# The widths of a mixture-of-experts layer's first product in steps of 16 slots instead of 32

## The chip, the cores and the metric

The kernel runs on 1 core of one Trainium2 chip. The metric is the device time of one execution in microseconds (us). Before the change three runs gave 1121.9, 1123.8 and 1128.33 us, with a median of 1123.8 us.

## The reference

The reference has two layers on x of 4 x 512 tokens with 512 channels. The first is a bidirectional recurrence with a time-dependent decay, a gated linear recurrence on its result, and a projection. The second is the same kind of conditioning followed by a mixture of 8 experts. Cut to what matters here:

```python
C = ceil(1.25 * S * K / E)            # 640 slots for each expert
probs = softmax(xr @ Wg)
gate_vals, expert_idx = top_k(probs, 2)
pos = running number of the token within its expert
kept = pos < C
dispatched = xr[dispatch_mask]        # 8 x 640 x 512
h = relu(einsum('ecd,edf->ecf', dispatched, w1))   # to 2048 hidden
expert_out = einsum('ecf,efd->ecd', h, w2)
x = x + the tokens' expert rows, weighted by their gates
```

An expert's slots beyond its number of tokens are empty. That number is known only when the kernel runs.

## The kernel before, in words

The first part of the program (`conditioning_and_routing`) computes the first layer, the conditioning and the routing for the four sequences, writes the tokens' rows into a DRAM tensor `slots` of 640 rows for each expert, and leaves each expert's number of tokens, limited to 1 to 640, in `counts`. It ends at about 370 us.

The second part (`experts`) is a loop over the 8 experts that every engine runs for itself, with semaphores between them. The hidden dimension of 2048 is cut into 16 blocks of 128. Matrices of fp32 are split into a high and a low part of type fp32r, and each product is made of three: high by high, low by high, high by low.

PE's program (`tensor_program`) is what the change touches. Within the loop over experts (L1624) it loads the expert's count into a register (L1625), and then runs a loop of 8 passes (L1630), each for two hidden blocks:

- `up` (first product, L1575 to L1577): 4 slices of the channels by 3 products into the PSUM tensor `ps_h`, for as many slots as the chosen width has. With up to 512 slots it is one body of 12 products; above, the slots are done in two parts of which the first has 320 columns, 24 products in all.
- `down` (second product, L1595 to L1597) of the hidden block before, for each tile of 128 slots that has tokens: 3 products of 512 columns into `ps_y`. It waits for the relu and the split of the hidden block, which ACT (L1702) and DVE (L1774) make. Tiles 0 and 1 are always done, tiles 2 to 4 behind a branch each (L1602).
- from the third pass on, four transposes of a tile of the next expert's rows (L1545).

The width is not a register operand of the product. PE chooses one of the bodies that the program holds, one for each width in `WIDTHS`, by nested branches on the count (`choose`, L1580 to L1587): the lower half stands behind the branch and is reached by falling through, the upper half by a jump. All bodies stand in the program one after the other, twice, since `up` is called twice in a pass. The chosen width is the smallest one that holds the count.

ACT and DVE read `ps_h` over fixed widths: 512 columns for up to 512 tokens, twice 320 for more. They also split the weights (L1676, L1679, L1734, L1737), that SP loads in pieces of 1 MB. POOL adds the finished rows into the output (L1524).

The lines that decide the bodies are:

```python
WIDTHS = range(2 * P, CAP + 1, P // 4)      # P = 128, CAP = 640
middle = (len(widths) - 1) // 2
with pe.If(count < widths[middle] + 1):
    choose(widths[:middle + 1])
with pe.Else():
    choose(widths[middle + 1:])
```

Of the kernel before, what the change touches and what calls it, by code (L numbers as in the profile page):

```python
# [24 lines left out]
P = 128  # L25
# [4 lines left out]
CAP = math.ceil(1.25 * B * T * TOPK / NE)  # L30
# [46 lines left out]
def build_program(nc, x, fside, cond, w1c, u1c, W_in, b_in, W_decay, b_decay, W_gate, b_gate,  # L77
# [3 lines left out]
    with ExitStack() as ctx:  # L81
# [18 lines left out]
        with ExitStack() as phase:  # L100
            first = conditioning_and_routing(nc, ctx, phase, ident, counts, count_sem, rows, cond_buffers, place0, load_sems,
                                     slots, out_rows, x, fside, cond, w1c, u1c,
                                     W_in, b_in, W_decay, b_decay, W_gate, b_gate, W_out, b_out,
                                     decay_bias, w2c, u2c, Wg, w1, w2)
        second = experts(nc, ctx, ident, counts, rows, count_sem, place0, load_sems, slots, out_rows, w1, w2)
        block = ctx.enter_context(nc.Block())

# [1298 lines left out]
def experts(nc, ctx, ident, counts, rows, s_count, place0, load_sems, slots, out_rows, w1, w2):  # L1406
# [32 lines left out]

    WIDE = 512  # L1440
    HALF = CAP // 2
    WIDTHS = range(2 * P, CAP + 1, P // 4)
    TURN_FROM = 2

    EVEN_ORDER, ODD_ORDER = (2, 4, 0), (3, 1)
# [88 lines left out]
    def tensor_program(pe):  # L1534
# [27 lines left out]
        def up(hidden, j, count):  # L1562
# [17 lines left out]
            def choose(widths):  # L1580
                if len(widths) == 1:
                    products(widths[0])
                    return
# [5 lines that stand above are left out]
            pe.wait_ge(s_wl1, hidden + 1)  # L1589
            choose(WIDTHS)  # L1590

# [235 lines left out]
```

How the kernel before makes its waits and increments, by code:

```python
    def wait(self):  # L69
        self.eng.wait_ge(self.sem, self.base + self.n)
# [207 lines left out]
    def sync_program(sp):  # L278
# [6 lines left out]
        def store(b):  # L285
            sp.wait_ge(s_ev_x2, TT * (b + 1))
            sp.dma_start(out_rows[b * T:(b + 1) * T].rearrange("(i p) c -> p i c", p=P), x_rows).then_inc(s_x2_out, 16)
# [4 lines left out]
        def clear_slots(first, last):  # L292
            for e in range(first, last):
                sp.dma_start(slots[e * CAP:(e + 1) * CAP, :].rearrange("(p i) c -> p i c", i=ST),
                             r2_rows[:, 0:1, :].to_broadcast([P, ST, ROW])).then_inc(s_init, 16)
        for h in range(2):
            half = slice(h * C // 2, (h + 1) * C // 2)
            sp.dma_start(f_rows[:, :, half], fside[0].rearrange("(i p) c -> p i c", p=P)[:, :, half]).then_inc(s_f_in if h else s_f_half, 16)
        sp.wait_ge(s_vec, 16 * N_VEC)
        load_x(0)
        sp.wait_ge(s_f_tp, CT)
        load_f(1)
        for n in range(4):
            load_w(n)
        sp.dma_start(wg[:], Wg.rearrange("(t p) e -> p t e", p=P)).then_inc(s_w, 16)
        sp.wait_ge(s_x_tp, CT)
        load_x(1)
        sp.wait_ge(s_f_tp, 2 * CT)
        load_f(2)
        sp.wait_ge(s_template, 2)
        clear_slots(1, NE + 1)
        sp.wait_ge(s_f_tp, 3 * CT)
        load_f(3)
        store(0)
        sp.wait_ge(s_x2_out, 16)
        load_x(2)
        store(1)
        sp.wait_ge(s_x2_out, 32)
        load_x(3)
        sp.wait_ge(s_bwd, 2 * (unit_no(1, B - 2, 1) + 1))
        sp.wait_ge(s_eukv, unit_no(1, B - 2, 1) + 1)
```

## Time and profile before

| | |
|---|---|
| runs | 1121.9, 1123.8, 1128.33 us; median 1123.8 |
| the profiled execution | 1130.62 us, span 1128.8 us |
| granted TensorE clock, mean over the span | 0.969 |
| PE busy | 1040.3 us (92%), 5034 products |
| PE weight loads busy (beside PE) | 816.5 us |
| DVE, ACT, POOL busy | 644.6, 519.7, 279.3 us |
| loop over experts | from 373.9 us to about 1109 us |

The span runs from the first to the last instruction of the profiled execution. A product's duration includes the time in which it overlaps the next one, so the rate of products is read from the distance between their starts. PEld is the loading of weights into the array, which overlaps the products. PEldq and PEq are the queue of PE: branches and register operations are shown there with their durations, and are not counted as busy time. "issue" is time in which an engine waited for nothing that the profile shows. The instruction queues (q8, q14) carry the program itself to the engines.

### The profile page before, as it was taken

What the parts mean: (1) busy time and instruction counts of PE and PEld (TensorE: products, weight loads), DVE (VectorE), ACT (ScalarE), POOL (GpSimd) and SP (SyncE); (2) the same over time, 40 slices, a digit from 0 to 9 for tenths busy, and PEclk for the clock granted to TensorE, in tenths of its full rate; (3) what the DMA queues carried; (4) which work ended last, traced back from release to release, by engine and by line L of the source; (5) the groups of instructions that cost most, each with busy time, mean ns of one, the idle gap of its engine ahead of it and who ended that gap; (6) DMA issues with size and microseconds to landing.
All of it is one profiled execution on the core that took longest, in us unless ns stands there. A gap on an engine that the chain in (4) does not pass through costs nothing.

```text
span 1128.8 us, 17219 instructions
## 1 busy us (share of the span) xinstructions
PE 1040.3 (92%) x5034; PEld 816.5 (72%) x5035; DVE 644.6 (57%) x939; ACT 519.7 (46%) x836; POOL 279.3 (25%) x232
## 2 busy tenths in 40 slices
PE   3599997999996899999999999999999999999993
PEld 2334543454455799989998999898887888899892
DVE  5899999999982333343334333555564344334551
ACT  6776774677632233343334333445553334334441
POOL 4665748634654000030002000300203002000202
PEclk9999898999988899999999999999999999999997
DMA  6991432224414422262226222634536225222521
GB/s 212 315 308 30 112 72 89 53 69 113 136 39 169 146 74 74 74 167 75 74 74 168 74 74 74 172 144 166 165 114 213 74 74 158 89 92 90 137 74 22
DMA packets 67104, 131.34 MB, mean 116 GB/s; under 512 B 4966, under 2 KB 6026, under 8 KB 67080
## 3 DMA queue, kind: packets, MB, share of 16 engines
q1 hardware_dynamic: 53856, 105.25, 26.8%
q0 software_dynamic: 13008, 25.52, 11.5%
q10 hardware_dynamic: 216, 0.28, 0.1%
q8 instruction: 12, 0.20, 0.1%
q14 instruction: 12, 0.10, 0.0%
HBM read 90.66 MB, written 35.22 MB: 112 GB/s over the span
## 4 chain that ended last, share of the span: by engine, by line
PE 64%; issue 1%; POOL 1%; DVEq 0%; DVE 0%; ACT 0%; POOLq 0%
PE ps_y L1595 11%; PE ps_y L1596 11%; PE ps_y L1597 11%; PE ps_h L1575 10%; PE ps_h L1576 10%; PE ps_h L1577 10%; PE ps_t L1545 1%; POOL out_dram L1524 1%; DVEq L1650 0%; DVE y L1797 0%; DVE hl L1774 0%; ACT y L1719 0%; DVE gate L1759 0%; DVEq L1773 0%; DVEq L1763 0%
## 5 line engine op out<-in xcount | busy, mean ns | idle before, releaser
L1575 PE MATMUL ps_h<-xh,w1h 128*128 128x320 f32 (+4 forms) x768 | 245.0, 319 | 7.7 <-issue 7.1
L1576 PE MATMUL ps_h<-xl,w1h 128*128 128x320 f32 (+4 forms) x768 | 241.3, 314 | 0.0
L1577 PE MATMUL ps_h<-xh,w1l 128*128 128x320 f32 (+4 forms) x768 | 241.2, 314 | 0.0
L1524 POOL DMA_INDIRECT out_dram<-y,token x40 | 63.8, 1594 | 642.4 <-DVE y L1797 402.2
L1774 DVE SCALAR_TENSOR_TENSOR hl<-ps_h,hh 128x320 fp32r<-128x320 f32 (+1 forms) x192 | 107.2, 558 | 191.9 <-ACT hh L1702 187.1
L1595 PE MATMUL ps_y<-w2h,hh 128*128 128x512 f32 x528 | 207.1, 392 | 0.8 <-issue 0.5
L1596 PE MATMUL ps_y<-w2h,hl 128*128 128x512 f32 x528 | 206.3, 391 | 0.0
L1597 PE MATMUL ps_y<-w2l,hh 128*128 128x512 f32 x528 | 206.1, 390 | 0.0
L1702 ACT ACTIVATE hh<-ps_h 128x320 fp32r<-128x320 f32 (+1 forms) x192 | 94.2, 491 | 234.6 <-PE ps_h L1577 231.2
L1737 DVE TENSOR_TENSOR w2l<-raw,w2h 128x512 fp32r<-128x512 f32 x127 | 87.8, 692 | 196.6 <-ACT w2h L1679 195.6
L1679 ACT ACTIVATE w2h<-raw 128x512 fp32r x127 | 80.1, 631 | 210.2 <-PE ps_y L1597 210.2
L515 PE MATMUL ps_mm<-ratios,wm 128*128 128x512 f32 x372 | 168.5, 607 | 7.2 <-DVE xT L1218 4.0
L1575 PEld LDWEIGHTS ps_h<-xh,w1h 128*128 128x128 f32 x768 | 145.5, 190 | 16.2 <-issue 10.5
L1576 PEld LDWEIGHTS ps_h<-xl,w1h 128*128 128x128 f32 x768 | 145.6, 190 | 5.0
L1577 PEld LDWEIGHTS ps_h<-xh,w1l 128*128 128x128 f32 x768 | 145.4, 189 | 2.6
L515 PEld LDWEIGHTS ps_mm<-ratios,wm 128*128 128x128 f32 x372 | 70.6, 195 | 91.5 <-issue 84.8
L1597 PEld LDWEIGHTS ps_y<-w2l,hh 128*128 128x128 f32 x528 | 99.1, 188 | 21.6
L1595 PEld LDWEIGHTS ps_y<-w2h,hh 128*128 128x128 f32 x528 | 99.2, 188 | 20.0 <-issue 2.7
L1596 PEld LDWEIGHTS ps_y<-w2h,hl 128*128 128x128 f32 x528 | 99.2, 188 | 17.0
L1734 DVE TENSOR_TENSOR w1l<-raw,w1h 128x512 fp32r<-128x512 f32 x127 | 87.6, 690 | 16.0 <-ACT w1h L1676 12.2
L1676 ACT ACTIVATE w1h<-raw 128x512 fp32r x127 | 79.2, 623 | 0.0
L1161 DVE TENSOR_TENSOR_SCAN sums_odd<-ps_decay,sums_odd 128x511 f32<-128x511 f32 x32 | 38.3, 1257 | 4.5 <-ACT sums_odd L791 4.5
(206 smaller groups left out, 1163.8 us busy)
## 6 DMA issues: line engine op xcount, KB each, us to landing
raw<-in_L_ffn_w_dram SPq DMA_DIRECT2D x64, 1024.0 KB
slots<-r_rows SPq DMA_DIRECT2D x8, 1302.5 KB, 22.6
rows<-slots SPq DMA_DIRECT2D x7, 1302.5 KB
rows<-in_x_dram SPq DMA_DIRECT2D x4, 1024.0 KB, 5.2
sums_even<-eukv POOLq DMA_DIRECT2D x8, 512.0 KB, 5.1
sums_odd<-eukv POOLq DMA_DIRECT2D x8, 512.0 KB, 5.3
out_dram<-rows SPq DMA_DIRECT2D x4, 1024.0 KB
f_rows<-in_fside_BxSxS_dram SPq DMA_DIRECT2D x3, 1024.0 KB, 6.6
```

The lines of the kernel that those rows point to most:

```text
L515: last = nc.tensor.matmul(ps_mm[:, k % 3, :], wm[:, m, dt, e * P:(e + 1) * P], ratio_of(0, b)[:, dt], start=(dt == 0), stop=(dt == CT - 1))
L1575: nc.tensor.matmul(o, w1h[:, j, dt, :], xh[:, dt, lo:hi], start=(dt == 0), stop=False)
L1576: nc.tensor.matmul(o, w1h[:, j, dt, :], xl[:, dt, lo:hi], start=False, stop=False)
L1577: last = nc.tensor.matmul(o, w1l[:, j, dt, :], xh[:, dt, lo:hi], start=False, stop=(dt == CT - 1))
L1595: nc.tensor.matmul(ps_y[:, i, :], hh[:, j, tok], w2h[:, j], start=first, stop=False)
L1596: nc.tensor.matmul(ps_y[:, i, :], hl[:, j, tok], w2h[:, j], start=False, stop=False)
L1597: return nc.tensor.matmul(ps_y[:, i, :], hh[:, j, tok], w2l[:, j], start=False, stop=last)
L1679: a.activation(w2h[:, (j + 1) % 2], raw2[:, bass.ds((c + (j + 1) // FC) % 2, 1), (j + 1) % FC] .rearrange("p o n -> p (o n)"), ACT.Copy).t ...
L1702: a.activation(hh[:, j % 2, lo:hi], ps_h[:, bank, 0:hi - lo], ACT.Relu).then_inc(s_hh, 1 if wide else 2)
L1734: v.tensor_tensor(w1l[:, j % 2], raw1[:, bass.ds((c + j // 2) % 2, 1), :, (j + 2) % FC * P:((j + 2) % FC + 1) * P] .rearrange("p o t q -> ...
L1737: v.tensor_tensor(w2l[:, (j + 1) % 2], raw2[:, bass.ds((c + (j + 1) // FC) % 2, 1), (j + 1) % FC] .rearrange("p o n -> p (o n)"), w2h[:, ( ...
L1774: v.scalar_tensor_tensor(out=hl[:, j % 2, lo:hi], in0=ps_h[:, bank, 0:hi - lo], scalar=0.0, in1=hh[:, j % 2, lo:hi].bitcast(F32), op0=ALU.max,
```

## The change

```diff
     WIDE = 512
     HALF = CAP // 2
-    WIDTHS = range(2 * P, CAP + 1, P // 4)
+    WIDTHS = range(2 * P, CAP + 1, P // 8)
     TURN_FROM = 2
```

The widths were 256, 288, ..., 640 (13) and are now 256, 272, ..., 640 (25). Only PE's program changes; those of DVE, ACT, POOL and SP are the same instruction by instruction.

PE's program at the head of the loop of 8 passes, where the search through the widths begins (L1585) and the first bodies stand. Before:

```order
L1630 UNCONDITIONAL_BRANCH
L1630 ISA
L1585 COMPARE_AND_BRANCH x4
L1570 REGISTER_ALU
L1575 MATMUL ps_h<-xh,w1h 128x256
...
L1585 UNCONDITIONAL_BRANCH
L1570 REGISTER_ALU
L1575 MATMUL ps_h<-xh,w1h 128x288
```

With the change:

```order
L1630 UNCONDITIONAL_BRANCH
L1630 ISA
L1585 COMPARE_AND_BRANCH x5
L1570 REGISTER_ALU
L1575 MATMUL ps_h<-xh,w1h 128x256
...
L1585 UNCONDITIONAL_BRANCH
L1570 REGISTER_ALU
L1575 MATMUL ps_h<-xh,w1h 128x272
```

One more branch stands ahead of the narrowest body, and the second body has 272 columns where it had 288.

The wide bodies, where 544 is the narrowest of them before and 528 after: the second part of the body (its first part has 320 columns). Before:

```order
L1577 MATMUL ps_h<-xh,w1l 128x320
L1568 REGISTER_ALU
L1575 MATMUL ps_h<-xh,w1h 128x224
L1576 MATMUL ps_h<-xl,w1h 128x224
L1577 MATMUL ps_h<-xh,w1l 128x224
```

With the change:

```order
L1577 MATMUL ps_h<-xh,w1l 128x320
L1568 REGISTER_ALU
L1575 MATMUL ps_h<-xh,w1h 128x208
L1576 MATMUL ps_h<-xl,w1h 128x208
L1577 MATMUL ps_h<-xh,w1l 128x208
```

The second part has 208 columns where it had 224, and a body with 224 stands behind it as one of its own. The whole of PE's program has 792 rows of different neighbours before and 1240 after.

## Rows read from the trace of the kernel before

**Rows 1.** The page: busy time by engine, and one line of the DMA queues.

```profile
PE 1040.3 (92%) x5034; PEld 816.5 (72%) x5035; DVE 644.6 (57%) x939; ACT 519.7 (46%) x836; POOL 279.3 (25%) x232
q8 instruction: 12, 0.20, 0.1%
```

**Rows 2.** The table by stretches: us, busy us (count) by engine, granted clock, DMA share, GB/s.

```profile
0.00:373.90 373.90, 310.04 (x1006) 164.92 (x1007) 322.28 (x421) 233.12 (x328) 211.60 (x178) 0.93 0.46 136
787.10:850.20 63.10, 61.64 (x356) 54.04 (x357) 38.15 (x60) 33.73 (x56) 8.67 (x8) 1.00 0.51 163
850.20:939.80 89.60, 89.59 (x404) 73.96 (x404) 37.88 (x59) 33.80 (x56) 8.59 (x7) 1.00 0.37 119
939.80:1046.70 106.90, 106.90 (x646) 96.75 (x646) 44.16 (x75) 39.20 (x74) 9.23 (x8) 1.00 0.33 105
```

**Rows 3.** Waits of PE, 370 to 1105 us: total us, times, longest.

```profile
PE ps_h L1575 <- issue: 7.1, 7, 3.3
```

**Rows 4.** Groups of L1575 by shape, 373.9 to 1109 us: busy us, mean ns, idle before.

```profile
L1575 PE MATMUL ps_h<-xh,w1h 128*128 128x512 f32 x64 | 25.5, 398 | 1.2 <-issue 1.2
L1575 PE MATMUL ps_h<-xh,w1h 128*128 128x352 f32 x64 | 21.2, 331 | 0.3 <-issue 0.3
L1575 PE MATMUL ps_h<-xh,w1h 128*128 128x288 f32 x64 | 19.4, 303 | 1.2 <-issue 1.2
L1575 PE MATMUL ps_h<-xh,w1h 128*128 128x224 f32 x64 | 17.4, 272 | 0.0
```

**Rows 5.** The timeline of PE: start us, us; bodies of 12 products by their ends.

```profile
796.87 0.29 PE L1575 MATMUL ps_h<-xh,w1h 128*128 128x288 f32 x1
798.45 0.39 PE L1595 MATMUL ps_y<-w2h,hh 128*128 128x512 f32 x1
...
866.65 0.39 PE L1595 MATMUL ps_y<-w2h,hh 128*128 128x512 f32 x1
869.37 0.39 PE L1575 MATMUL ps_h<-xh,w1h 128*128 128x512 f32 x1
...
962.78 0.30 PE L1575 MATMUL ps_h<-xh,w1h 128*128 128x320 f32 x1
964.53 0.27 PE L1575 MATMUL ps_h<-xh,w1h 128*128 128x224 f32 x1
965.86 0.40 PE L1595 MATMUL ps_y<-w2h,hh 128*128 128x512 f32 x1
```

**Rows 6.** Branches of the search, L1585: 377.9 to 380.9, then 385.5 to 1105 us.

```profile
L1585 PEldq COMPARE_BRANCH  x3: 215/217/2618, 377.9 to 380.8; - x3
L1585 PEldq COMPARE_BRANCH  x458: 65/202/215, 385.7 to 1101.7; - x153
```

**Rows 7.** Three searches (L1585) and the weight loads they lead to (L1575).

```profile
L1585 PEldq COMPARE_BRANCH  x3: 202/202/215, 488.9 to 489.4; - x3
L1575 PEld LDWEIGHTS ps_h<-xh,w1h x3: 188/188/188, 490.8 to 491.8; 128*128 128x128 f32 x3
...
L1585 PEldq COMPARE_BRANCH  x3: 202/202/208, 656.1 to 656.6; - x3
L1575 PEld LDWEIGHTS ps_h<-xh,w1h x1: 190/190/190, 658.3 to 658.3; 128*128 128x128 f32 x1
...
L1585 PEldq COMPARE_BRANCH  x4: 65/71/208, 798.2 to 798.6; - x4
L1575 PEld LDWEIGHTS ps_h<-xh,w1h x2: 188/188/188, 800.3 to 800.8; 128*128 128x128 f32 x2
```

**Rows 8.** The timeline of PE: the fifth expert's first product.

```profile
787.13 0.39 PE L1575 MATMUL ps_h<-xh,w1h 128*128 128x288 f32 x1 [1.06 <-issue]
```

**Rows 9.** Instruction queues in 360 to 470 us, then in 470 to the end.

```profile
q8 instruction: 4, 0.07, 0.2%
...
q14 instruction: 1, 0.01, 0.0%
```

**Rows 10.** The timeline of PE behind the long branch.

```profile
381.17 0.42 PE L1575 MATMUL ps_h<-xh,w1h 128*128 128x320 f32 x1 [0.86 <-issue]
```

## The prediction

> **What bounds the kernel now.** I read the page first: PE is busy 92% of the span, DVE 57%, ACT 46% [rows 1]. The table by stretches shows where: from 373.9 us on, where the experts run, PE is busy in practically every microsecond (89.59 of 89.6 in the stretch of the sixth expert) at a granted clock of 1.00, and DVE and ACT have half their time left [rows 2]. So a product that becomes shorter there shortens the kernel, and an instruction of PE's queue costs something only where the queue runs late. The waits of PE show that this is rare now: 7.1 us ahead of L1575, all of it "issue", in 7 places [rows 3].
>
> **Which products change.** Routing the reference's own inputs gives the eight experts 626, 770, 788, 326, 267, 495, 518 and 306 tokens, and 640 is the cap. The trace agrees: beside the 320 columns of most experts it has 64 products of each kind at 352, 288, 512 and 224 columns, 224 being the second part of 544 [rows 4]. In steps of 16 the widths become 336 for 326, 272 for 267, 496 for 495 and 528 for 518 (second part 208). 626, 770 and 788 stay at 640 and 306 at 320. Each of the four has 16 hidden blocks of 12 products that become 16 columns narrower, 192 products.
>
> What a column is worth I take from starts, since durations are pipelined. Twelve products of 512 columns go from 866.65 to 869.37, 226.7 ns each; twelve of 320 from 962.78 to 964.53, 145.8 ns; twelve of 288 from 796.87 to 798.45, 131.7 ns [rows 5]. From 288 to 512 that is 0.42 ns a column, so 6.7 ns for 16. Twelve of 224 take 964.53 to 965.86, 110.8 ns, where the line would give 105: a floor begins to show. For 208 columns I bound the saving by nothing and by 6.7 ns and take 2 ns. Sum: 3 x 192 x 6.7 ns + 192 x 2 ns = 4.3 us saved (3.9 to 5.2).
>
> **What is added on PE's queue.** The search through the widths is nested branches. By the code 640 takes three jumps now and four after; 352 and 288 have four steps and 336 and 272 five; 320 has one step more, 544 three and 528 five, 512 and 496 four both. A step that falls through takes 65 to 71 ns, one that jumps 202 to 217 ns [rows 6, 7], with some 60 ns between them. The Trainium skill (Advanced Engine Details and Errata, Control Flow Timing) gives about 108 ns for a compare-and-branch; the rows show two prices around it, and the sum by 108 ns would be lower by under 1 us. Mostly this lies beside PE's work: in the fifth expert the last branch of a search ends at 798.8 and the LDWEIGHTS that it leads to starts at 800.3; in the third expert these are 656.8 and 658.3 [rows 7]. That is 1.5 us of lead in both, so a longer search costs nothing in the steady loop. It costs where PE already waits for "issue", as the 1.06 us ahead of 787.13 [rows 8]: about seven such places by 0.13 to 0.4 us, +2 us (1 to 3).
>
> **The size of the loop.** Here the change is largest. A narrow body is 26 instructions (a register operation, twelve LDWEIGHTS and MATMUL pairs, a branch), a wide one 51. Before, a search has nine narrow and four wide bodies and 12 compares, 450 instructions; after, seventeen, eight and 24, 874. The loop over pairs of hidden blocks has two searches and 188 other instructions: 1088 before, 1936 after, and the loop over experts around it 1144 and 1992.
>
> The trace shows how PE's instructions come. Queue 8 moves 12 packets in 0.20 MB, 16.4 KB each [rows 1]; 4 of them lie between 360 and 470 us, where the loop over experts is first run, and none between 470 and the end, where only queue 14 has one [rows 9]; so 8 came before 360. Ahead of 373.9 us PE has some 1006 products [rows 2], so about 2,060 instructions with waits: about 257 to a packet. That makes the loop over experts 4.5 packets before and 7.8 after. Before, what was fetched once stayed: no packet comes on queue 8 in the last 650 us. And the fetch runs one ahead: packets come in the first pass at blocks that are entered without a stall, except where a jump overtakes them. That is the one branch of 2618 ns, between 377.9 and 380.9 [rows 6]; at ordinary 213 ns this is a stall of 2.4 us, of which PE lost 0.86 us idle plus a slow start, 1.0 us [rows 10]. All 458 later branches of a search stay at 215 ns or below [rows 6].
>
> After the change the inner loop begins in the ninth packet of PE's program and ends in the sixteenth, eight packets, and on entering its last one the fetch ahead asks for the seventeenth, a ninth. How many are kept no row says; the rows show six (five of the loop and one ahead). Nine at once is half as much again as anything the trace shows to be kept, and nothing suggests a loss or a gain below that. The price of a loss is the branch of 2618 ns. I take that nine aren't kept and that the ninth takes the place of the first, which the jump back needs in every pass.
>
> The Trainium skill (Runtime: NRT & Kernel Launch, Instruction fetch mechanics) gives PE 128 KiB, 2048 instructions, refilled in blocks of 16 KiB, and says a taken branch outside what is held stalls for a fetch. By it nine blocks don't fit. The trace agrees with the block (16.4 KB) and with the stall (2618 ns), and not with the page's sentence that only two blocks are held: five are jumped among without a fetch.
>
> **The sum for that case.**
> - Each of 56 jumps back within an expert: 2.4 us less the lead of 1.5 us [rows 7] = 0.9 us, 50 us.
> - The lead itself is eaten by the longer searches: 3 experts x 7 x 0.27 us, 3 x 7 x 0.13 and 7 x 0.4, 11 us.
> - Seven changes of expert: at the five after wide or 512-column experts and the like the lead is 489.6 to 490.8, 1.2 us [rows 7], so 1.2 us each; the two after narrow ones have none [rows 8], 2.4 us each: 11 us.
> - The first pass: both searches of the first expert now hop over several packets within 0.3 us of each other. Two stalls of 2.4 us before the very first product stand free (4.8); two more in the second search less the 1.4 us that PE's queue covered before, 3.4 instead of 1.0: +7 us.
> - Products -4.3 us, starts of experts +2 us.
>
> Together 77 us: 1130.6 of the profiled execution becomes 1208. The shown median is 1123.8, 6.8 below that execution; from it I forecast **1201 us**. Bounds of this case: if only the wide experts lose their first block, the jumps give half, +40, 1164; if a miss takes 3.4 us because the packet has not been asked for ahead, +1 us in 63 places, 1264.
>
> DVE, ACT, POOL and SP keep their instructions, and read ps_h over the same columns as before. The weights' transfers lie beside PE's work with 33 to 51% of the DMA engines busy [rows 2]; a slower PE only gives them more room. I cost these at nothing.
>
> **Rivals.**
> 1. *All blocks stay.* Then only the saving, the starts and the first pass count: -4.3 + 2 + 0 to 7, 1121.5 to 1128.5, likeliest 1127. For it: before, not one packet was fetched twice. It decides the sign: it holds if nine packets of 16.4 KB are kept, or if a packet asked for ahead never displaces one in use. Chance 0.35.
> 2. *Every block is lost in turn*, because the oldest goes first: each of the 32 passes of the wide experts pays about what the first does (7 us) and the narrow ones some more. +150 to +400, about 1375. Against it: queue 8 would have to run hundreds of times. Chance 0.12.
> 3. *The shorter products win outright*: no loss of blocks, no cost of the first pass or the searches, and 208 columns on the line: -5.2 us, 1118.6; to pass the 0.5% (5.6 us, about what a measurement of this kernel can tell from no change) it needs luck besides. That the change picks other widths than I read is in here too: with one expert fewer it saves 1.3 us less. Chance 0.03.
>
> **How the numbers follow.** The case of the displaced first block has 0.50, and its time is the prediction. Slower by over 0.5%: 0.50 + 0.12 + 0.08 (the first rival with a dear first pass) = 0.70. Within 0.5%: the rest of the first rival, 0.27. Faster: 0.03. The range must take in the first rival and leave out the second: 1119 to 1264. The likeliest case's own is 1164 to 1264.
>
> **What would show it.** Queue 8 with some 140 packets instead of 12, two in a pass of about 14 us; the jump back (L1630) or the first compare behind it (L1585) at 2.4 us or more once in every pass; PE idle for "issue" by about 80 us in 60 places; products at 336, 272, 496 and 208 columns, 64 of each kind. Queue 8 at 15 or 16 packets and branches at 217 ns or less in the steady loop would prove the first rival, and my forecast wrong in the step "nine aren't kept"; the first pass and the durations of the fifth to seventh expert (63.1, 89.6, 106.9 us now [rows 2]) would then show the rest of the sum alone. A clock below 1.00 in the experts would be a cost that I have not counted.

## The result and the profile after

The changed kernel takes 1534.3 us (four runs, 1499.0 to 1565.6) against 1125.9 us; the ratio to the kernel before is 1.339, with a 95% interval of 1.333 to 1.345. The ratio is formed from the two shorter of the four runs (1499.0 and 1515.7 us) only, and the profiled execution is one of the two longer (1552.9 us), so counts and times below are somewhat above those of the median.

The page of the changed kernel: busy time by engine, the granted clock in 40 slices, and the instruction queue of PE.

```profile
span 1551.1 us, 17347 instructions
...
PE 1150.8 (74%) x5034; PEld 899.5 (58%) x5035; DVE 639.5 (41%) x939; ACT 519.7 (34%) x836; POOL 279.1 (18%) x232
...
PEclk9999999986799968998679999997777878887798
...
q8 instruction: 235, 3.85, 1.1%
```

The number of products is the same as before, DVE, ACT and POOL are busy for as long as before or slightly less [rows 1], and queue 8 has 235 packets instead of 12. PE's waits in the loop over experts, of the changed kernel:

```profile
PE ps_h L1575 <- issue: 302.6, 66, 15.2
PE ps_y L1595 <- DVE hl L1774: 16.3, 9, 2.4
```

PE idles 302.6 us for "issue" ahead of its first products where it idled 7.1 [rows 3], 295 us more. It is also busy 110.5 us longer (1150.8 against 1040.3) for no more work, at a mean granted clock of 0.864 instead of 0.969. The two make 406 of the 422 us by which the span grew. The second line is a wait for DVE's split of the hidden block, 16.3 us, that was 0.3 us before; it lies in the sixth and seventh expert, where PE stalls most, and what makes it wasn't looked for.

The table by stretches of the changed kernel, one row for each expert (us, busy us and count by engine, granted clock, DMA share, GB/s):

```profile
362.50:545.20 182.70, 129.27 (x648) 116.30 (x646) 46.27 (x79) 40.31 (x75) 4.87 (x6) 0.84 0.20 69
545.20:716.40 171.20, 128.00 (x644) 115.58 (x644) 44.06 (x74) 39.22 (x73) 8.34 (x8) 0.86 0.22 67
716.40:900.90 184.50, 130.44 (x644) 117.59 (x644) 44.00 (x74) 39.22 (x73) 8.24 (x8) 0.84 0.21 62
900.90:970.00 69.10, 66.58 (x353) 59.90 (x354) 35.24 (x53) 31.92 (x53) 5.78 (x6) 0.95 0.42 124
970.00:1032.00 62.00, 60.36 (x357) 52.91 (x356) 37.95 (x58) 33.66 (x57) 8.62 (x7) 1.00 0.52 165
1032.00:1239.10 207.10, 127.82 (x409) 95.19 (x407) 40.94 (x63) 35.95 (x60) 11.89 (x10) 0.78 0.24 71
1239.10:1465.50 226.40, 136.11 (x644) 119.23 (x644) 43.18 (x72) 38.96 (x73) 5.49 (x6) 0.79 0.16 46
1465.50:1530.00 64.50, 62.06 (x332) 55.47 (x331) 31.89 (x49) 26.99 (x47) 7.03 (x6) 0.97 0.31 82
```

The loss is not spread evenly. The experts with 336, 272 and 320 columns (rows four, five and eight) run within about a microsecond of before: the fifth takes 62.0 us where it took 63.1 [rows 2]. The four wide experts and the one with 496 columns take 1.5 to 2.3 times as long. The packets of queue 8 lie with them. The queue in 716.4 to 900.9 us (the third expert), in 900.9 to 1032 (the fourth and fifth) and in 1032 to 1239.1 (the sixth):

```profile
q8 instruction: 30, 0.49, 1.1%
...
q8 instruction: 1, 0.02, 0.0%
...
q8 instruction: 71, 1.16, 2.8%
```

The seventh (1239.1 to 1465.5) has 72, the first two 29 and 23. A count of the program's instructions in blocks of 256, from the ninth packet on, gives the reason. The narrow experts jump only among the first bodies of each search, so they enter three or four blocks in a pass; with the block behind each one that is entered, six or seven are wanted. The sixth expert enters five, the seventh six and the wide ones seven, and with the blocks behind them that is nine for each.

Two passes of the loop show the two kinds of refetch. The queue, the searches (L1585) and the jump back (L1630) in 610 to 626 us, in the second expert, then from 1104.3 to 1130.5, in the sixth:

```profile
q8 instruction: 2, 0.03, 0.9%
L1585 PEldq COMPARE_BRANCH  x8: 202/208/325, 620.1 to 625.4; - x8
L1630 PEldq COMPARE_BRANCH  x1: 3540/3540/3540, 616.3 to 616.3; - x1
...
q8 instruction: 9, 0.15, 2.7%
L1585 PEldq COMPARE_BRANCH  x8: 65/154/4282, 1108.5 to 1122.5; - x8
L1630 PEldq COMPARE_BRANCH  x1: 3906/3906/3906, 1104.4 to 1104.4; - x1
```

In the first, two packets come and only the jump back stalls. In the second nine come, in an expert that enters five blocks and has those behind them asked for: all nine are fetched again in each pass.

### The profile page after: what moved, and what is told of

Same layout as the page of the kernel before. It is cut to its first block, busy times and chain, and to the rows that moved or that the text cites. A ratio compares the mean times of both kernels' runs of the same rounds, so it can differ in the third digit from the quotient of the medians.

```text
span 1551.1 us, 17347 instructions
## 1 busy us (share of the span) xinstructions
PE 1150.8 (74%) x5034; PEld 899.5 (58%) x5035; DVE 639.5 (41%) x939; ACT 519.7 (34%) x836; POOL 279.1 (18%) x232
## 4 chain that ended last, share of the span: by engine, by line
PE 54%; issue 20%; DVE 1%; ACT 1%; POOL 0%; DVEq 0%; ACTq 0%; POOLq 0%
PE ps_h L1575 11%; PE ps_h L1576 9%; PE ps_h L1577 9%; PE ps_y L1595 8%; PE ps_y L1596 8%; PE ps_y L1597 8%; PE ps_t L1545 1%; DVE hl L1774 1%; ACT hh L1702 0%; POOL out_dram L1524 0%; DVE w1l L1734 0%; ACT y L1719 0%; ACT w1h L1676 0%; DVEq L1734 0%; ACTq L1701 0%
## 5 line engine op out<-in xcount | busy, mean ns | idle before, releaser
L1575 PE MATMUL ps_h<-xh,w1h 128*128 128x320 f32 (+4 forms) x768 | 286.8, 373 | 302.6 <-issue 302.6
L1575 PEld LDWEIGHTS ps_h<-xh,w1h 128*128 128x128 f32 x768 | 176.2, 229 | 330.6 <-issue 325.2
L1576 PE MATMUL ps_h<-xl,w1h 128*128 128x320 f32 (+4 forms) x768 | 276.4, 360 | 0.0
L1577 PE MATMUL ps_h<-xh,w1l 128*128 128x320 f32 (+4 forms) x768 | 274.0, 357 | 0.0
L1595 PE MATMUL ps_y<-w2h,hh 128*128 128x512 f32 x528 | 213.0, 403 | 24.2 <-DVE hl L1774 16.3
L1596 PE MATMUL ps_y<-w2h,hl 128*128 128x512 f32 x528 | 210.9, 399 | 0.0
L1597 PE MATMUL ps_y<-w2l,hh 128*128 128x512 f32 x528 | 209.7, 397 | 0.0
L1576 PEld LDWEIGHTS ps_h<-xl,w1h 128*128 128x128 f32 x768 | 177.2, 231 | 5.2
L1577 PEld LDWEIGHTS ps_h<-xh,w1l 128*128 128x128 f32 x768 | 175.6, 229 | 4.3
L532 PE MATMUL ps_mm<-z_gate,wm 128*128 128x512 f32 x72 | 36.6, 640 | 4.6 <-DVE z_gate L1213 4.6
```

The lines of the kernel that those rows point to most:

```text
L1575: nc.tensor.matmul(o, w1h[:, j, dt, :], xh[:, dt, lo:hi], start=(dt == 0), stop=False)
L1576: nc.tensor.matmul(o, w1h[:, j, dt, :], xl[:, dt, lo:hi], start=False, stop=False)
L1577: last = nc.tensor.matmul(o, w1l[:, j, dt, :], xh[:, dt, lo:hi], start=False, stop=(dt == CT - 1))
L1595: nc.tensor.matmul(ps_y[:, i, :], hh[:, j, tok], w2h[:, j], start=first, stop=False)
L1596: nc.tensor.matmul(ps_y[:, i, :], hl[:, j, tok], w2h[:, j], start=False, stop=False)
L1597: return nc.tensor.matmul(ps_y[:, i, :], hh[:, j, tok], w2l[:, j], start=False, stop=last)
```

## The experiments

All were compared with the kernel before on the same chips (1124.8, 1126.3 and 1125.7 us in the three groups).

**The same bodies twice.** It does the products of before with the search and the size of the change.

```diff
-    WIDTHS = range(2 * P, CAP + 1, P // 8)
+    WIDTHS = sorted([*range(2 * P, CAP + 1, P // 4), *range(2 * P, CAP, P // 4)])
```

> 25 bodies, but with the 13 widths of before: every width except 640 stands twice, and the first of the two is taken. PE does the products of before, with the search and nearly the program of the change: the loop of 8 passes has 1886 instructions (1088 before, 1936 with the change), which is again eight blocks of 256 and a ninth asked for ahead. Theory A (PE's instruction memory doesn't hold nine blocks at once, oldest or least used goes): slow like the change, 1450 to 1570 us, over 150 packets on queue 8. Theory B (the longer search itself costs): slow as well. Theory C (products of 336, 272, 496 and 208 columns run worse, or let the clock fall): like before, 1122 to 1130 us, queue 8 at 16 packets or fewer.

Measured: 1776.9 us (1672 to 1798). Its page, the instruction queue:

```profile
q8 instruction: 347, 5.69, 1.4%
```

The narrower products are out as a cause: with the old widths it is even slower, and the clock falls as well (0.818 over its profiled execution). It doesn't tell the length of the search from the size of the loop. It also lies above the 1570 us that I had allowed. The three narrow experts are spared here too (2 packets in all), but the first three wide ones have 64, 72 and 58 packets where the change has 29, 23 and 30: they stay in the kind of pass that fetches nine. Why they do here and not in the change is open.

**Only the six widths in use.**

```diff
-    WIDTHS = range(2 * P, CAP + 1, P // 8)
+    WIDTHS = (272, 320, 336, 496, 528, 640)
```

> Only the six widths that these inputs use with the change: 272, 320, 336, 496, 528, 640. The products are those of the change, the search has two or three steps, the loop of 8 passes has 610 instructions, three blocks. Theories A and B: faster than before by the 4.3 us of the narrower products and some 1 to 3 us at the starts of experts and in the first pass, 1117 to 1123 us, 5 or fewer packets on queue 8 after 360 us. Theory C: slow, over 1400 us.

Measured: 1118.2 us, ratio 0.995 (0.994 to 0.997), 10 packets on queue 8 in all. The products of the change, without its program, are 0.5% faster than the kernel before.

**Twenty bodies.** The five widths left out are none of those in use.

```diff
-    WIDTHS = range(2 * P, CAP + 1, P // 8)
+    WIDTHS = [n for n in range(2 * P, CAP + 1, P // 8) if n not in (368, 384, 400, 432, 464)]
```

> The change without the widths 368, 384, 400, 432 and 464: 20 bodies, the products of the change for all eight experts, four or five steps in the search as in the change, but a loop over experts that ends in the seventh block, so that with the block asked for ahead eight are wanted. Theory A with room for eight blocks: no refetch, 12 to 16 packets on queue 8, and before less 4.3 us plus up to 7 us of first pass, 1119 to 1129 us. Theory A with room for only seven: slow, over 1300 us. Theory B (length of the search): slow like the change, 1450 us or more.

Measured: 1136.7 us, ratio 1.010 (1.007 to 1.012). The queue of the whole execution, the second expert, and the first expert's waits for "issue" on the timeline of PE:

```profile
q8 instruction: 14, 0.23, 0.1%
...
496.80:610.60 113.80, 113.50 (x646) 103.25 (x645) 44.17 (x74) 39.23 (x74) 8.44 (x7) 1.00 0.32 96
...
374.60 0.63 PE L1575 MATMUL ps_h<-xh,w1h 128*128 128x320 f32 x1 [7.72 <-issue]
377.11 0.63 PE L1575 MATMUL ps_h<-xh,w1h 128*128 128x320 f32 x1 [1.35 <-issue]
388.37 0.64 PE L1575 MATMUL ps_h<-xh,w1h 128*128 128x320 f32 x1 [5.30 <-issue]
```

There is no refetch: 14 packets for a longer program, none of them after the first expert, and the wide second expert takes 113.8 us, as before the change. With four or five steps in the search, as in the change, the search is out as the cause of the 400 us. The step of theory A holds: seven blocks and one ahead stay. The time is above the 1129 us that I had allowed. In the profiled execution the first pass alone makes it slower than before, dearer than I had put it: 7.72 + 1.35 + 5.30 = 14.4 us of idle time where the kernel before has 3.29 us, in the line below, and the 0.86 us of [rows 10].

```profile
373.93 0.63 PE L1575 MATMUL ps_h<-xh,w1h 128*128 128x320 f32 x1 [3.29 <-issue]
```

**The width chosen once for each expert.** The branches stand around the loop of passes instead of inside it, so there are 25 such loops; what `choose` calls for a width is `passes(width)`.

```diff
             pe.wait_ge(s_wl1, hidden + 1)
-            choose(WIDTHS)
+            products(width)
...
+            def passes(width):
+                with pe.Fori(0, FT // 2) as q:
...
+            choose(WIDTHS)
             down(e * FT + (FT - 1), 1, count, last=True)
```

> All 25 widths, but the width is chosen once for each expert, and each of the 25 bodies is a loop of 8 passes of its own. PE's program grows to some 25 blocks or more, but the loop that runs has one or two. Theory A: what counts is the loop that runs and not the program: no refetch in the steady loop, some 2 to 4 packets for each expert that jumps to a new body, 1119 to 1140 us. Theory D (the size of the whole program counts): slow, over 1300 us. Theory B: fast, since the search leaves the inner loop.

Measured: 1252.0 us, ratio 1.112 (1.109 to 1.115), 67 packets. PE's waits in its loop over experts, and the second expert's first product:

```profile
PE ps_h L1575 <- issue: 116.0, 8, 23.8
...
529.84 0.63 PE L1575 MATMUL ps_h<-xh,w1h 128*128 128x320 f32 x1 [23.82 <-issue]
```

My expectation was half right. Counted with each product and its weight load as two, PE's program has some 7,900 instructions against 3,400 with the change, and yet the steady loop has next to no wait: all of this idle time lies in 8 places, one for each expert, and only 4.4 us more lie elsewhere. So the size of the whole program isn't what counts. But I had expected 2 to 4 packets for each new body and at most 1140 us, and there were up to 11 packets: each of the five steps of the search now jumps over several blocks, every one is a fetch that only the one before it reveals, and PE stands idle for 23.8 us. A search over far bodies costs one fetch for each step.

**Twenty bodies, shifted.** 132 instructions that never run stand ahead of the loop of passes.

```diff
+            with pe.If(count < 2):
+                for n in range(65):
+                    nc.tensor.matmul(ps_t[:].rearrange("p t q -> p (t q)"), w1h[:, 0, n % CT], w2h[:, 0], start=True, stop=True)
             with pe.Fori(0, FT // 2) as q:
```

> The kernel with 20 bodies, with 132 instructions of PE that never run (65 products behind a branch on fewer than 2 tokens) between the head of the loop over experts and the loop of 8 passes. Nothing that runs is changed except one more branch in each expert. The loop of 8 passes has the same 1666 instructions, but its end now lies a few dozen instructions inside the sixteenth block of 256 instead of in the fifteenth, so that with the block ahead nine are wanted instead of eight. Theory A (blocks held, eight at most): the wide experts refetch, 1250 to 1700 us and over 100 packets on queue 8. Theory E (the number of instructions in the loop counts, not where they lie): like the unshifted kernel, 1131 to 1139 us.

Measured: 2147.4 us, ratio 1.906 (1.902 to 1.911), against 1136.7 for the same loop 132 instructions earlier. Its queue, the longest search branch, and the first, fourth and fifth expert:

```profile
q8 instruction: 510, 8.36, 1.9%
...
L1585 PEldq COMPARE_BRANCH  x592: 65/219/6702, 368.4 to 2113.5; - x198
...
365.00:639.10 274.10, 148.82 (x648) 133.74 (x647) 45.39 (x77) 39.94 (x75) 3.19 (x5) 0.73 0.15 48
1187.20:1400.80 213.60, 104.11 (x356) 83.02 (x356) 38.33 (x57) 34.41 (x56) 5.51 (x6) 0.70 0.19 56
1400.80:1464.30 63.50, 60.60 (x353) 53.83 (x353) 35.45 (x55) 31.95 (x53) 6.55 (x6) 0.97 0.38 117
```

This is the clearest of the experiments: what runs is the same but for one branch for each expert, and the time nearly doubles. It isn't the number of instructions in the loop but the number of blocks that it wants, by where it lies. My expectation of up to 1700 us was too low, since narrow experts now pay as well: the fourth takes 213.6 us. Counted as above, it now enters six blocks and wants nine, and has 72 packets; the fifth enters four or five, wants seven or eight, has one packet and takes 63.5 us. The blocks behind those entered have to be in the count: the sixth expert of the change enters only five blocks and refetches, the wide ones with twenty bodies unshifted enter seven and don't.

**The kernel before, shifted alike.** The same edit to the kernel before.

> The kernel before, with the same 132 instructions that never run in the same place. It is the control for what the branch and the shift cost by themselves: with either theory the loop keeps to six or seven blocks with the one ahead, at most 14 packets on queue 8, 1124 to 1131 us.

Measured: 1130.0 us, ratio 1.004 (1.002 to 1.005), 13 packets. So the shift and its branch cost 3.7 us where the blocks have room, most of it in the first expert's first pass, and 1011 us where they haven't (2147.4 less 1136.7).

**850 instructions that never run, inside the loop.** The kernel before, with the loop of passes as long as in the change.

```diff
                 up(at, 0, count)
+                with pe.If(count < 2):
+                    for n in range(425):
+                        nc.tensor.matmul(ps_t[:].rearrange("p t q -> p (t q)"), w1h[:, 0, n % CT], w2h[:, 0], start=True, stop=True)
```

> The kernel before with 850 instructions that never run (425 products behind a branch on fewer than 2 tokens) between the first search and what follows it, inside the loop of 8 passes. The loop is as long as that of the change (1939 instructions, eight blocks from end to end), but three of its blocks are jumped over. Theory A in the form that only blocks that are entered, and the one behind each, are wanted: eight at most, no refetch in the steady loop, 1125 to 1140 us with a dearer first pass. Theory F (the distance from the loop's first to its last instruction counts): slow like the change, over 1400 us.

Measured: 1140.3 us, ratio 1.012 (1.010 to 1.014). The queue of the whole execution, all search branches, and the long wait of its first pass:

```profile
q8 instruction: 18, 0.29, 0.1%
...
L1585 PEldq COMPARE_BRANCH  x464: 65/202/3112, 370.1 to 1115.5; - x155
...
386.90 0.63 PE L1575 MATMUL ps_h<-xh,w1h 128*128 128x320 f32 x1 [10.63 <-issue]
```

No refetch after the first passes (from 405 us on one packet comes): the distance from the loop's first to its last instruction doesn't matter. The loop spans eight blocks and enters five at most, seven with those behind; the blocks jumped over take no room.

**Thirteen bodies with the widths of the change.** Nine narrow and four wide, as before.

```diff
-    WIDTHS = range(2 * P, CAP + 1, P // 8)
+    WIDTHS = (272, 304, 320, 336, 368, 416, 464, 496, 512, 528, 576, 608, 640)
```

> 13 bodies as before, nine narrow and four wide, so a loop of the same length and a search of the same kind, but with the widths 272, 304, 320, 336, 368, 416, 464, 496, 512, 528, 576, 608, 640. The products are those of the change for all eight experts. Theory A and B: before less the 4.3 us of the narrower products, and nothing else, 1118 to 1122 us, queue 8 at 12 packets. Theory C (narrower products are no gain): 1124 us or more.

Measured: 1123.6 us against 1126.3, ratio 0.997 (0.996 to 0.999), 12 packets. This falls between my two cases (up to 1122, or 1124 and more); the stretches tell more than the whole. The fourth to seventh expert (336, 272, 496 and 320 with 208 columns), each from its first product to the next one's, and two products of 208 columns, the second and the twelfth of one body:

```profile
716.70:783.80 67.10, 65.68 (x357) 58.15 (x355) 37.68 (x58) 33.97 (x57) 7.51 (x7) 1.00 0.50 149
783.80:845.60 61.80, 60.44 (x357) 52.93 (x357) 38.14 (x59) 33.70 (x56) 8.46 (x8) 1.00 0.52 167
845.60:934.20 88.60, 88.60 (x404) 73.98 (x404) 37.94 (x59) 33.73 (x56) 8.45 (x7) 1.00 0.38 121
934.20:1041.10 106.90, 106.90 (x645) 96.75 (x645) 44.27 (x75) 39.18 (x74) 9.11 (x8) 1.00 0.33 105
...
936.16 0.27 PE L1576 MATMUL ps_h<-xl,w1h 128*128 128x208 f32 x1
937.28 0.28 PE L1577 MATMUL ps_h<-xh,w1l 128*128 128x208 f32 x1
```

This is the term for the products by itself. The fifth, sixth and seventh expert took 63.1, 89.6 and 106.9 us before [rows 2], the fourth 68.4: for the fourth to the seventh the gains are 1.3, 1.3, 1.0 and 0.0 us, 3.6 in all. From the second to the twelfth start of 208 columns it is 1.12 us, 112 ns a product. The same ten starts of 224 columns in the kernel before take 1.12 us as well (964.63 to 965.75): the seventh expert gains nothing.

**Seven widths close to the counts.**

```diff
-    WIDTHS = range(2 * P, CAP + 1, P // 8)
+    WIDTHS = (268, 306, 326, 496, 518, 626, 640)
```

> Seven widths laid close to the eight counts of these inputs: 268, 306, 326, 496, 518, 626, 640. Against the kernel with six widths, 192 products each of the eighth expert lose 14 columns, of the fourth 10, of the fifth 4, of the first 14 (its second part), of the seventh 10 (its second part, 198 columns, where 208 and 224 already took the same time). At 0.42 ns a column that is 1.1 + 0.8 + 0.3 + 1.1 + 0 = 3.3 us. If the columns are what bounds these products: 1114 to 1117 us, against 1118.2 of the six widths. If a width that is no multiple of 16 costs something, or the wait has moved elsewhere: 1118 us or more.

Measured: 1119.3 us against 1125.7, ratio 0.994 (0.991 to 0.996). I had expected 1114 to 1117 us. The interval overlaps that of the six widths, so the further gain isn't shown by the times. Both short lists beat both kernels, on these inputs; they are laid to these counts, and a list for other inputs would have to be laid anew.

## Why the prediction was wrong

**What failed.** The forecast was slower by 77 us with a 0.50 chance; it is slower by 408 by the medians of all runs. The mechanism was in the prediction: PE's instruction memory doesn't hold nine blocks at once. The twenty bodies, shifted and not, and the 850 dead instructions bear this out, and the doubled bodies agree: eight stay, nine don't. The places where PE idles are about as many as forecast, 66 against some 60, but each costs 4.6 us (302.6 by 66) instead of 1.3. The steps that failed are two: what a ninth block displaces and what a miss costs in idle time, and the clock, which the sum left out.

1. *"The ninth takes the place of the first, which the jump back needs"*, one stall in a pass. It does so in the narrower of the two patterns, the passes with two packets. But in all 16 passes of the sixth and seventh expert (71 packets in the sixth) and in one to three early passes of each wide expert ahead of them, seven to ten packets come in each pass, and PE idles for 10 to 11 us of it. The pass of the sixth expert at 1104.4, from one jump back to the next, lasts 27.50 us, of them 17.65 busy, and each of the five branches that jump to another block stalls in it, for 3.2 to 6.4 us:

```profile
1104.40:1131.90 27.50, 17.65 (x54) 13.17 (x53) 4.60 (x7) 3.98 (x7) 0.00 (x0) 0.75 0.27 82
```

   That was my second rival, every block lost in turn, with 0.12 and 1375 us (150 to 400 us more). It had the mechanism for these experts and was too low too: it priced a pass at about 7 us, for the wide experts, and the sixth expert only at "some more", where its 207.1 us are 14.7 us a pass above the 89.6 of before.

   The passes with one displaced block are dearer than forecast as well. From 595.2 to 671.6 us the second expert makes four of them in 21.1, 16.7, 21.6 and 17.0 us, on average 4.5 us above the 14.6 of before; the sum had 0.9 us for the stall and 0.3 for the eaten lead. The jump back takes 3.54 and 3.63 us in the shorter ones, but 5.92 and 6.17 in the longer, and never the 2.6 us that I took. I took that from the only one in the trace of before, which had been asked for ahead: its packet starts 0.3 us behind the branch, at 378.4 us, while those of these jumps start 1.0 us behind it (617.2 us) or 3.5 (598.7 us). My upper bound used 3.4 us.

2. *The clock.* I priced stalls by idle time alone and named a lower clock only as a cost that I hadn't counted. Two of these passes show what it does, from one jump back to the next, in the changed kernel:

```profile
595.20:616.30 21.10, 17.29 (x83) 15.60 (x82) 4.86 (x9) 4.64 (x10) 0.00 (x0) 0.84 0.27 100
616.30:633.00 16.70, 14.96 (x86) 13.37 (x85) 5.70 (x10) 4.90 (x10) 0.00 (x0) 1.00 0.08 21
```

and one pass of the kernel before:

```profile
512.50:527.10 14.60, 14.60 (x83) 13.25 (x83) 4.83 (x9) 4.61 (x10) 0.00 (x0) 1.00 0.39 141
```

The pass at 616.3 is nearest to the case that I forecast: two packets, one stall, full clock, PE idle for 1.74 us, and 2.1 us more than the 14.6 of before. The pass at 595.2 has the same products and costs 6.5 us more than before. 3.8 of these are idle time behind the longer jump. The other 2.7 are the clock: the granted clock averages 0.84, since behind the gap of 3.8 us 19 products of 320 columns start 0.267 us apart, the rate of 1.2 GHz, and the later ones 0.147 us apart, that of 2.4 GHz. Behind the gap of 1.74 us they keep the 0.147. So PE is busy 17.29 us for work that took 14.60. Over the kernel the longer busy time is 110 us of the 422. The longer idle gaps of PE cost more here than their own length.

**What held.** The products: 4.3 us forecast, 3.6 measured. 0.42 ns a column held for 336 and 272 and nearly for 496; for 208 columns my saving of 2 ns a product was too much, since they take the 112 ns of 224. Four experts get narrower products, as read from the counts. POOL and the weights' transfers cost nothing; behind DVE PE waits 16.3 us that I had put at nothing. The longer search costs nothing in the steady loop: the second expert takes 113.8 us with twenty bodies and, from 491.0 to 604.8 us, before. The sum gave each of the 56 jumps back its stall, and those of the three narrow experts have none, because the blocks between their bodies aren't entered; only my lower bound, 1164 us, allowed for that.

**A term too small.** The first pass: +7 us forecast. With twenty bodies it costs 10 us of idle time more than before, and with the lower clock behind these gaps some 13: from the head of the loop over experts to the second start of it are 130.4 us, of them 116.0 busy, against 117.2 and 113.1 in the kernel before. The kernel before with 850 dead instructions has a like wait, 10.63 us at once. That alone would have made the change slower than before even had every block stayed. I had given this rival mostly to "within 0.5%" (0.27 of its 0.35); its time would have been about that of the twenty bodies, 1137 us, 1% slower.

**On the chances.** The range ended at 1264 us, since I left the second rival out of it. The trace held one stall, and no row on what happens when room runs out; a range over such an unknown should have held that rival.

**What stays open.** Why a wide expert falls from nine packets a pass to two (the third expert has passes of both kinds), why the jump back takes 3.5 us in one of its passes and 6 in the next, and why the time spreads over 4% from run to run, isn't explained. By my reckoning neither "the oldest goes" nor "a fixed place for each block" gives both patterns, but no run tried the rule of replacement by itself. That the block behind each entered one counts is read from the count of blocks and the packets of each expert; no experiment was made for it alone.

## What to carry to other kernels

Count the instruction blocks that a loop enters on each engine, with the one behind each, before giving it more specialised bodies; the number in the trace to watch is the packets of the instruction queues after the first pass, which should be next to none. A loop that is near the limit can be tipped over by code ahead of it that never runs, so measure a change of size with a control that shifts the code and changes nothing else. Few bodies laid where the sizes are do more than many at even steps, and a search belongs near its bodies.

## What the runs showed of the hardware that I had not expected

- A shift by 132 instructions took the same loop from 1136.7 to 2147.4 us. Eight blocks of 16.4 KB, the one behind each that is entered included, stay with PE (twenty bodies, 14 packets in all); with a ninth there are 510 packets.
- The refetch isn't a gentle loss: up to nine or ten packets a pass, with branches of up to 6.7 us, where one block was too many.
- Blocks that are jumped over take no room (850 dead instructions inside the loop, 18 packets).
- Where the first block is no longer held, the jump back takes 3.2 to 6.5 us in the changed kernel. Five such jumps in a chain leave PE idle for 23.8 us at the start of an expert in the kernel that chooses once.
- An idle gap of 3.8 us was followed by 19 products at half the rate, one of 1.7 us by none.
- Products of 208 and of 224 columns take the same time, 112 ns from start to start.
